# A state-space block on one core: B and C from one 128-row product, one of delta's casts moved to ScalarE

## Chip, cores and metric

One NeuronCore of one Trainium2 chip runs the whole program. The metric is device time in microseconds (us) of one execution.

## What is computed

Input x is 4 batches x 2048 tokens x 256 channels. Cut to what the change touches, with 512 inner channels and 64 states:

```python
xn    = layernorm(layernorm(x)) ; xi, z = split(xn @ W_in)
u     = silu(causal_conv4(xi) + conv_b)
x_dbl = u @ W_xproj                     # 16 + 64 + 64 columns
dt_r, B, C = x_dbl[:, :16], x_dbl[:, 16:80], x_dbl[:, 80:144]
delta = softplus(dt_r @ W_dt + b_dt)
h_t   = h_{t-1} * exp(delta_t * A) + (delta_t * u_t) B_t ;  y_t = h_t . C_t
out   = x + (y + u * D) * silu(z) @ W_out   # then a second residual block
```

## The kernel before

Four stages follow one another, each a block of five instruction streams that meet at its end: norm, **project** (the one that changes), scan, output. The scan reads from DRAM what the project stage stored.

The project stage (`project_stage`, from L343) walks over 16 tiles of 512 tokens (four per batch). `over_tiles` writes four tiles into a hardware loop over the first three batches and writes the last four out after it. All streams work on several tiles at once:

- **SyncE** issues every store. One `step` does `turn_stores` (the parts of delta*u, five stores of 1 MiB, L468; the parts of B, 0.5 MiB, L471; C, 0.25 MiB, L474), then `front_stores` (silu(z) and u, 1 MiB each), then `back_stores` (eight stores of 0.5 MiB of delta's three bf16 parts, L459), which waits for `d3_done` of the tile before. That is 11.75 MiB per tile.
- **TensorE**: per tile eight column blocks of `W_in` (`front`, L503) alternate with transposes of delta*u and B (`turn`, L537); then `back`: the 16 rows of dt_r (L510), four products with `W_dt` (L520), and two products of 128 rows (L510 again). The first of these has B twice, the second C twice, because `w_x` holds the columns of B and of C two times.
- **ScalarE** empties PSUM: `xi` (L576), turned parts (L624, L630), silu(z) (L579), u (L586), dt_r (L597), v (L601); then softplus's functions over 2048 columns: Abs (L604), Exp (L606), Ln (L608), the last two each behind a table load; last the copies `b_in` (L611) and `c_out` (L614).
- **VectorE**: `softplus` (L675 to L687), the convolution of the tile two ahead (`front`, L659 and L662), then `split`: x is cut into three bf16 parts, by cast, subtract, cast, subtract, for delta (into `dparts`) and then for delta*u (into `uparts`); then `split_b` the same for B. L675 is the first operation of a tile, and it waits for Exp of that tile (L606) and for `d3_done`.

Below, T*n* is the start of L675 of tile *n*, and T*n*+x a moment x us later.

Of the kernel before, what the change touches and what calls it, by code (L numbers as in the profile page):

```python
# [22 lines left out]
ALU = mybir.AluOpType  # L23
# [5 lines left out]
P = 128  # L29
# [7 lines left out]
TW = 512  # L37
# [305 lines left out]
def project_stage(nc, d, xnT):  # L343

    with ExitStack() as ctx:  # L345
# [6 lines left out]
        w_in = sb("p_w_in", [P, KD, 2 * DI])  # L352
        w_x = sb("p_w_x", [P, MI, RANK + 4 * NS])
        w_dt = sb("p_w_dt", [RANK, DI])
# [7 lines left out]
        dtr = sb("p_dtr", [RANK, TW])  # L362
        b_in = sb("p_b_in", [P, TW])
# [3 lines left out]
        c_out = sb("p_c_out", [P, TW])  # L367
        u_turn = sb("p_u_turn", [P, PARTS, SUB, DI])
# [42 lines left out]
        turns_stored = [sem(f"turns_stored{j}") for j in range(4)]  # L411
        n_weights = 10

# [19 lines left out]
        def _(sp):  # L433
            wx = d["W_xproj"].rearrange("(m p) n -> p m n", p=P)
            sp.dma_start(w_in[:, :, :], d["W_in"].rearrange("(k p) n -> p k n", p=P)).then_inc(weights, 16)
            sp.dma_start(w_x[:, :, 0:RANK], wx[:, :, 0:RANK]).then_inc(weights, 16)
            for r in range(4):
                at, frm = RANK + NS * r, RANK + NS * (r // 2)
                sp.dma_start(w_x[:, :, at:at + NS], wx[:, :, frm:frm + NS]).then_inc(weights, 16)
            sp.dma_start(w_dt[:, :], d["W_dt"]).then_inc(weights, 16)  # L440
# [50 lines left out]
            sp.wait_ge(dparts_stored, 16 * NCB * (NT + 1))  # L491
            sp.wait_ge(c_stored, 16 * (NT + 1))
            for j in range(4):
# [3 lines left out]
        def _(pe):  # L497
# [9 lines left out]
            def back(i, c, b):  # L507
                def rows(bank, lo, n):
                    for m in range(MI):
                        last = nc.tensor.matmul(bk_bank[0:n, bank, :], w_x[:, m, lo:lo + n], u[:, c % 2, m, :],  # L510
                                                start=(m == 0), stop=(m == MI - 1))
                    last.then_inc(back_ready, 1)

                pe.wait_ge(u_ready, i * 4 + 8)
                pe.wait_ge(back_read, i * 7 + 7)
                rows(2, 0, RANK)
                for m in range(MI):

                    pe.wait_ge(back_read, i * 7 + (8, 8, 9, 10)[m])
# [37 lines left out]
        def _(act):  # L557
            act.sem_inc(in_read, 2)
            act.sem_inc(back_read, 7)
            act.sem_inc(u_ready, 4)  # L560
# [8 lines left out]
            def front(i, m):  # L569
# [19 lines left out]
            def step(i, c, b, ahead1, ahead2):  # L589
# [4 lines left out]
                if ahead1:  # L594
                    middle(*ahead1)
                act.wait_ge(back_ready, i * 7 + 1)
                nc.scalar.activation(dtr[:, :], bk_bank[0:RANK, 2, :], ACT.Identity).then_inc(back_read, 1)  # L597
                act.wait_ge(delta_done, i + 1)
                for m in range(MI):
                    act.wait_ge(back_ready, i * 7 + 2 + m)  # L600
                    nc.scalar.activation(v[:, m, :], bk_bank[:, (3, 2)[m % 2], :], ACT.Identity,  # L601
                                         bias=b_dt[:, m:m + 1]).then_inc(back_read, 1)
                act.wait_ge(back_read, i * 7 + 12)
                nc.scalar.activation(ex[:, :, :], v[:, :, :], ACT.Abs).then_inc(abs_done, 1)  # L604
# [3 lines left out]
                nc.scalar.activation(lw[:, :, :], w1[:, :, :], ACT.Ln).then_inc(ln_done, 1)  # L608
                act.wait_ge(back_ready, i * 7 + 6)
                act.wait_ge(br_done, i + 1)  # L610
                nc.scalar.activation(b_in[:, :], bk_bank[:, 0, :], ACT.Identity).then_inc(back_read, 1)  # L611
                act.wait_ge(c_stored, i * 16 + 16)
                act.wait_ge(back_ready, i * 7 + 7)
                nc.scalar.activation(c_out[:, :], bk_bank[:, 1, :], ACT.Identity).then_inc(back_read, 1)  # L614

            def take_turn(i, g):
# [9 lines left out]
                else:  # L626
                    n, places = ((2, (0, 1, 2)), (1, (6, 7)))[g - 6]
                    for at in places:
                        src = turn_bank[:, g % 2, 0:n * SUB * P].rearrange("p (c s m) -> p s c m", s=SUB, m=P)
                        nc.scalar.activation(b_turn[:, :, at:at + 3 * n - 2:3, :], src[:, :, :, 0:NS],  # L630
                                             ACT.Identity).then_inc(turn_read, 1)

            for m in range(8):
                front(0, m)
            middle(0, 0, 0)
            over_tiles(act, step)
            for i in (NT, NT + 1):
                for g in range(8):
                    take_turn(i, g)

        @block.vector
        def _(dve):
            dve.sem_inc(delta_done, 1)
            nc.vector.memset(uparts[:, :, :, :], 0.0).then_inc(cleared, 1)
            nc.vector.memset(b_parts[:, :, :], 0.0).then_inc(cleared, 1)
            nc.vector.memset(dparts[:, :, :, :], 0.0).then_inc(cleared, 1)
            nc.vector.memset(c_out[:, :], 0.0).then_inc(cleared, 1)
            nc.vector.memset(xi[:, :, 0:TAPS - 1], 0.0).then_inc(xi_free, 1)
# [40 lines left out]
            def split(i):  # L689
                for src, rest, parts, free, first, whole, one, left, two, three, had in (  # L690
                        (lw, w1, dparts, (dparts_stored, i * (16 * NCB) + 16 * NCB), delta_done, i + 2, d1_done, dr_done,
                         d2_done, d3_done, 1),
                        (du, du, uparts, (turned, i * 8 + 16), du_done, i + 3, u1_done, ur_done, u2_done, u3_done, 2)):
                    dve.wait_ge(first, whole)
                    dve.wait_ge(*free)
                    nc.vector.tensor_copy(parts[:, 0], src[:, :, :]).then_inc(one, 1)
                    dve.wait_ge(one, i + 1)
                    nc.vector.tensor_tensor(rest[:, :, :], src[:, :, :], parts[:, 0], ALU.subtract).then_inc(left, 1)
                    dve.wait_ge(left, i + 1)
                    nc.vector.tensor_copy(parts[:, 1], rest[:, :, :]).then_inc(two, 1)  # L700
                    dve.wait_ge(two, i + 1)
                    nc.vector.tensor_tensor(parts[:, 2], rest[:, :, :], parts[:, 1], ALU.subtract).then_inc(three, 1)

            def split_b(i):
                dve.wait_ge(back_read, i * 7 + 13)
                dve.wait_ge(turned, i * 8 + 16)
                dve.wait_ge(b3_done, i + 2)
                nc.vector.tensor_copy(b_parts[:, 0], b_in[:, :]).then_inc(b1_done, 1)
                dve.wait_ge(b1_done, i + 1)
                nc.vector.tensor_tensor(b_rest[:, :], b_in[:, :], b_parts[:, 0], ALU.subtract).then_inc(br_done, 1)  # L710
                dve.wait_ge(br_done, i + 2)
                nc.vector.tensor_copy(b_parts[:, 1], b_rest[:, :]).then_inc(b2_done, 1)
                dve.wait_ge(b2_done, i + 1)
                nc.vector.tensor_tensor(b_parts[:, 2], b_rest[:, :], b_parts[:, 1], ALU.subtract).then_inc(b3_done, 1)

            def step(i, c, b, ahead1, ahead2):
# [4 lines left out]
                split(i)  # L721
                split_b(i)

            front(0, 0, 0)
# [739 lines left out]
```

## Time and profile before

| what | value |
|---|---|
| three runs, us | 5814.91, 5815.9, 5816.22 (median 5815.9) |
| profiled execution, us | 5813.2, of which the trace's span is 5811.4 |
| busy over the span | VectorE 95%, TensorE 90%, ScalarE 60%, GpSimd 39% |
| 50 to 850 us (holds the project stage) | VectorE 707 of 800 us, TensorE 675, ScalarE 563; DMA share 0.82 |
| 900 to 5400 us (inside the scan) | VectorE 4426 of 4500 us; DMA share 0.26 |

The DMA share is the mean busy share of the 16 DMA engines; where all work without a gap this profile shows 1.02 or 1.03. PEclk is the granted share of TensorE's 2.4 GHz. Rows of the order-of-time view read: start us, duration us, engine, line, operation, output and inputs, count, and in brackets the idle time before and what ended it.

### The profile page before, as it was taken

The page shows a single profiled execution, that of the slowest core. Times are in us where ns is not written, and L with a number is a line of the kernel's source. Part 1 is how long each engine was busy: PE and PEld are TensorE (multiplying, and loading weights), DVE is VectorE, ACT ScalarE, POOL GpSimd, SP SyncE. Part 2 cuts the span into 40 slices and gives each one's busy share as a digit, 9 for nine tenths or more (in the row PEclk, how much of TensorE's full clock was granted, in tenths as well). Part 3 has the DMA queues.
Part 4 walks back from the last instruction along what each step waited for, and adds up shares of the span by engine and source line. Part 5 has one row for each costly group of instructions (what it writes and reads, how often), then busy time and mean ns, then how long its engine had stood idle before and what let it go on. Part 6 is the DMA issues. An engine that isn't in the chain of part 4 may idle for free. (4 is left out here: it accounts for less than half of the span.)

```text
span 5811.4 us, 149606 instructions
## 1 busy us (share of the span) xinstructions
PE 5241.6 (90%) x38780; PEld 2478.7 (43%) x38780; DVE 5505.2 (95%) x3555; ACT 3494.6 (60%) x8238; POOL 2262.3 (39%) x6777
## 2 busy tenths in 40 slices
PE   5999779999999999999999999999999999997999
PEld 3344334444444444444444444444444444435666
DVE  5999989999999999999999999999999999995776
ACT  6777656666666666666666666666666666652333
POOL 2000034444444444444444444444444444440111
PEclk9999889999999999999999999999999999998999
DMA  7999942222222222222222222222222222224342
GB/s 245 332 321 337 344 111 53 54 54 55 54 52 53 54 54 54 54 52 53 54 54 55 54 52 53 54 55 54 54 52 54 53 55 54 54 44 147 115 141 73
DMA packets 1105518, 547.25 MB, mean 94 GB/s; under 512 B 753744, under 2 KB 1015056, under 8 KB 1105056
## 3 DMA queue, kind: packets, MB, share of 16 engines
q1 hardware_dynamic: 1093776, 533.89, 34.4%
q10 hardware_dynamic: 11664, 12.52, 0.6%
q8 instruction: 25, 0.41, 0.0%
q14 instruction: 53, 0.43, 0.0%
HBM read 296.83 MB, written 249.82 MB: 94 GB/s over the span
## 5 line engine op out<-in xcount | busy, mean ns | idle before, releaser
L997 DVE TENSOR_TENSOR_SCAN s_h<-s_decay,s_ubank 128x1024 f32<-128x1024 f32 x2048 | 4460.9, 2272 | 11.5 <-ACT s_ubank L962 11.2
L949 ACT ACTIVATE s_decay<-s_abank 128x512 f32<-128x512 f32 x4096 | 2210.4, 595 | 4.8 <-PE s_abank L887 1.4
L872 PE MATMUL s_ybank<-s_h,s_window 128*8 128x256 f32 x16416 | 1948.2, 602 | 1.9 <-DVE s_h L997 1.9
L913 PE MATMUL s_ubank<-s_x,s_w 128*128 128x256 bf16 x8192 | 1245.7, 275 | 375.5 <-DVE s_h L997 375.3
L1033 POOL TENSOR_TENSOR s_carry<-s_decay,s_h 128x64 f32<-128x64 f32 x2032 | 879.5, 433 | 1752.2 <-ACT s_decay L949 1576.4
L962 ACT ACTIVATE s_ubank<-s_seed 128x64 f32<-128x64 f32 x2048 | 478.3, 234 | 1703.2 <-PE s_ubank L913 1311.6
L887 PE MATMUL s_abank<-xnT,s_a 128*128 128x256 bf16 x8192 | 1254.9, 274 | 33.2 <-DMA s_w<-scratch_b_rows 30.1
L913 PEld LDWEIGHTS s_ubank<-s_x,s_w 128*128 128x128 bf16 x8192 | 675.7, 98 | 1197.7 <-DVE s_h L997 1096.5
L887 PEld LDWEIGHTS s_abank<-xnT,s_a 128*128 128x128 bf16 x8192 | 758.4, 98 | 195.8 <-ACT s_decay L949 35.7
L872 PEld LDWEIGHTS s_ybank<-s_h,s_window 128*8 128x8 f32 x16416 | 376.9, 97 | 839.6 <-issue 730.6
L1037 POOL TENSOR_TENSOR s_seed<-s_carry,s_first 128x64 f32<-128x64 f32 x2048 | 656.7, 321 | 164.3 <-ACT s_first L955 4.0
L1039 POOL TENSOR_TENSOR s_decay<-s_none 128x64 f32<-128x64 f32 x2048 | 617.3, 301 | 0.0
L503 PE MATMUL p_in<-xnT,p_w_in 128*128 (+1 forms) x512 | 252.4, 619 | 32.5 <-ACT p_xi L576 21.5
L1021 POOL TENSOR_TENSOR s_window<-s_c,s_none 64x32 f32<-64x32 f32 x512 | 129.9, 254 | 367.3 <-PE s_ybank L872 347.2
L1007 POOL MEMSET s_h<- 128x4096 f32 x1 | 3.5, 3511 | 663.6 <-POOLq L345 663.6
L1204 PE MATMUL o_gu<-o_xparts,o_wgu 128*128 128x512 bf16 x1152 | 257.8, 381 | 1.1 <-POOL o_xparts L1416 1.1
L897 PEld LDWEIGHTS s_firstbank<-s_x,s_w 128*128 128x128 bf16 x512 | 48.8, 95 | 444.0 <-issue 441.7
L1270 ACT ACTIVATE o_sg<-o_gu 128x512 f32<-128x512 f32 x96 | 57.4, 598 | 271.3 <-PE o_gu L1204 271.2
L510 PE MATMUL p_bk<-p_u,p_w_x 128*128 128x512 f32 (+1 forms) x384 | 203.4, 687 | 0.0
L955 ACT ACTIVATE s_first<-s_firstbank 128x256 f32<-128x256 f32 x512 | 203.3, 397 | 0.0
L939 ACT ACTIVATE s_y<-s_ybank 128x256 f32<-128x256 f32 x514 | 198.5, 386 | 6.8 <-PE s_ybank L872 6.8
L897 PE MATMUL s_firstbank<-s_x,s_w 128*128 128x512 bf16 x512 | 199.5, 390 | 2.0 <-DMA s_x<-scratch_u_rows 1.3
(135 smaller groups left out, 3098.2 us busy)
## 6 DMA issues: line engine op xcount, KB each, us to landing
s_x<-scratch_u_rows SPq DMA_DIRECT2D x4096, 32.0 KB
scratch_u_rows<-p_u_turn SPq DMA_DIRECT2D x90, 1024.0 KB, 6.6
scratch_delta_rows<-p_dparts SPq DMA_DIRECT2D x136, 512.0 KB, 6.2
xnT<-scratch_delta_rows SPq DMA_DIRECT2D x1024, 64.0 KB, 2.7
scratch_y<-s_y SPq DMA_DIRECT2D x1036, 16.0 KB
scratch_sz<-p_sz SPq DMA_DIRECT2D x16, 1024.0 KB, 6.2
scratch_u<-p_u SPq DMA_DIRECT2D x16, 1024.0 KB, 7.9
s_w<-scratch_b_rows SPq DMA_DIRECT2D x256, 64.0 KB, 2.4
```

Source lines behind the costliest of these rows:

```text
L503: last = nc.tensor.matmul(in_bank[:, m % 2, :], w_in[:, k, m * P:(m + 1) * P], xnT[:, k, bass.ds(i * TW, TW)], start=(k == 0), stop=(k == ...
L872: last = nc.tensor.matmul(y_bank[32 * ct:32 * ct + WIN, 1 - x, :], window[:, of, (at + t) * WIN:(at + t + 1) * WIN], H[:, 1 - x, :, t], st ...
L887: last = nc.tensor.matmul(a_bank[:, b, jj], a_w[:, half, j, :], x1[:, g, :, half, j, s * T:(s + 1) * T], start=True, stop=True)
L897: nc.tensor.matmul(first_bank[:, :, :], w2[:, g, 4 * s + 2 * x, :], x2[:, s, 0, 2 * x], start=True, stop=True).then_inc(first_ready, 1)
L913: last = nc.tensor.matmul(dst.rearrange("p q (a t) -> p a q t", t=2), w2[:, g, 4 * s + 2 * x + e, :], x2[:, s, :, 2 * x + e, q:q + 32, :], ...
L949: nc.scalar.activation(dst.rearrange("p x q t -> p q x t"), a_bank[:, b].rearrange("p j r (x t) -> p (j r) x t", x=2), ACT.Exp).then_inc(e ...
L962: nc.scalar.activation(u_bank[:, k % 2, :, 0], seed[:, k % CPS, :], ACT.Identity).then_inc(seeded, 1)
L997: nc.vector.tensor_tensor_scan(H[:, x, PT * p:PT * p + PT, :].rearrange("p q t -> p (q t)"), decay[:, x * (1 + c % 2), p].rearrange("p q t ...
L1033: nc.gpsimd.tensor_tensor(carry[:, k % CPS, :], decays, before, ALU.mult).then_inc(carried, 1)
L1037: nc.gpsimd.tensor_tensor(seed[:, k % CPS, :], carry[:, k % CPS, :], first[:, x, PT * p:PT * p + PT], ALU.add).then_inc(carried, 1)
L1039: nc.gpsimd.tensor_tensor(decays, none[:, :], none[:, :], ALU.mult).then_inc(carried, 1)
L1204: last = nc.tensor.matmul(gu[:, m % 2, r, :], wgu[:, r, kk, m * P:(m + 1) * P], xparts[:, part, kk, :], start=(n == 0), stop=(n == 3 * KD ...
```

## The change

`w_x` holds B and C once, so one product of 128 rows gives B in rows 0 to 63 and C in rows 64 to 127. One copy (`bc_in`) takes the place of `b_in` and `c_out`. C goes to DRAM twice from the upper 64 rows, 0.125 MiB each. The cast into `dparts[:, 1]` is done on ScalarE after the copies of v (`second_delta`), and the subtraction that reads it is the last operation of VectorE's tile (`split_last`). SyncE's `back_stores` waits for both. The weights come by 6 transfers in place of 10.

```diff
         w_x = sb("p_w_x", [P, MI, RANK + 2 * NS])
...
-            sp.dma_start(w_x[:, :, 0:RANK], wx[:, :, 0:RANK]).then_inc(weights, 16)
-            for r in range(4):
-                at, frm = RANK + NS * r, RANK + NS * (r // 2)
-                sp.dma_start(w_x[:, :, at:at + NS], wx[:, :, frm:frm + NS]).then_inc(weights, 16)
+            sp.dma_start(w_x[:, :, :], wx[:, :, :]).then_inc(weights, 16)
...
             def back_stores(i, c, b):
+                sp.wait_ge(d2_done, i + 1)
                 sp.wait_ge(d3_done, i + 1)
...
-                    sp.dma_start(d["C"][:, rows], c_out[:, :]).then_inc(c_stored, 16)
+                    for h in range(2):
+                        sp.dma_start(d["C"][h * NS:h * NS + NS, rows], bc_in[NS:P, :]).then_inc(c_stored, 16)
...
                 rows(0, RANK, 2 * NS)
-                rows(1, RANK + 2 * NS, 2 * NS)
...
+            def second_delta(i):
+                act.wait_ge(dr_done, i + 1)
+                nc.scalar.activation(dparts[:, 1], w1[:, :, :], ACT.Identity).then_inc(d2_done, 1)
...
+                second_delta(i)
+                act.wait_ge(back_read, i * 6 + 11)
                 nc.scalar.activation(ex[:, :, :], v[:, :, :], ACT.Abs).then_inc(abs_done, 1)
...
-                nc.scalar.activation(b_in[:, :], bk_bank[:, 0, :], ACT.Identity).then_inc(back_read, 1)
-                act.wait_ge(c_stored, i * 16 + 16)
-                act.wait_ge(back_ready, i * 7 + 7)
-                nc.scalar.activation(c_out[:, :], bk_bank[:, 1, :], ACT.Identity).then_inc(back_read, 1)
+                act.wait_ge(c_stored, i * 32 + 32)
+                nc.scalar.activation(bc_in[:, :], bk_bank[:, 0, :], ACT.Identity).then_inc(back_read, 1)
...
+            act.wait_ge(cleared, 4)
...
             for i in (NT, NT + 1):
                 for g in range(8):
                     take_turn(i, g)
+                if i == NT:
+                    second_delta(NT)
...
+            nc.vector.memset(w1[:, :, :], 0.0).then_inc(dr_done, 1)
...
+            def split_last(i):
+                dve.wait_ge(d2_done, i + 2)
+                nc.vector.tensor_tensor(dparts[:, 2], w1[:, :, :], dparts[:, 1], ALU.subtract).then_inc(d3_done, 1)
...
                 split(i)
                 split_b(i)
+                split_last(i)
```

**VectorE, the end of a tile**, before (L696 to L702 are the splits of delta and delta*u, L708 to L714 B's, L675 the next tile):

```order
L696 CAST p_dparts<-p_lw 128x2048
L698 TENSOR_TENSOR p_w<-p_lw,p_dparts 128x2048
L700 CAST p_dparts<-p_w 128x2048
L702 TENSOR_TENSOR p_dparts<-p_w,p_dparts 128x2048
L695 ISA
L696 CAST p_uparts<-p_du 128x2048
```

and the same engine and place with the change, where lines have moved (L723 is `split_last`, L679 the next tile's first operation):

```order
L696 CAST p_dparts<-p_lw 128x2048
L698 TENSOR_TENSOR p_w<-p_lw,p_dparts 128x2048
L700 ISA
L701 CAST p_uparts<-p_du 128x2048
L703 TENSOR_TENSOR p_du<-p_du,p_uparts 128x2048
L705 CAST p_uparts<-p_du 128x2048
L707 TENSOR_TENSOR p_uparts<-p_du,p_uparts 128x2048
L710 ISA
L713 CAST p_b_parts<-p_bc_in 128x512
L715 TENSOR_TENSOR p_b_rest<-p_bc_in,p_b_parts 128x512
L717 CAST p_b_parts<-p_b_rest 128x512
L719 TENSOR_TENSOR p_b_parts<-p_b_rest,p_b_parts 128x512
L723 TENSOR_TENSOR p_dparts<-p_w,p_dparts 128x2048
L679 TENSOR_SCALAR p_w<-p_ex 128x2048
```

One cast has gone, and the operation that completes `dparts` stands behind the other splits.

**ScalarE, from the last copy of v to the next tile**, with the change:

```order
L602 ACTIVATE p_v<-p_bk,p_b_dt 128x512
L580 ACTIVATE p_dparts<-p_w 128x2048
L605 REGISTER_ALU
L606 ACTIVATE p_ex<-p_v 128x2048
L608 ACT_TABLE_LOAD
L608 ACTIVATE p_ex<-p_ex 128x2048
L610 ACT_TABLE_LOAD
L610 ACTIVATE p_lw<-p_w 128x2048
L611 REGISTER_ALU
L614 ACTIVATE p_bc_in<-p_bk 128x512
```

The cast (L580) stands ahead of Abs and Exp; one copy follows Ln where there were two.

## Rows read from the trace of the kernel before

**Rows 1.** Order of time, VectorE, tile 2 and the start of tile 3

```profile
218.15 1.22 DVE L675 TENSOR_SCALAR p_w<-p_ex 128x2048 f32<-128x2048 f32 x1
...
238.43 1.23 DVE L696 CAST p_dparts<-p_lw 128x2048 bf16<-128x2048 f32 x1
...
242.02 1.23 DVE L700 CAST p_dparts<-p_w 128x2048 bf16<-128x2048 f32 x1
243.28 2.29 DVE L702 TENSOR_TENSOR p_dparts<-p_w,p_dparts 128x2048 bf16<-128x2048 f32 x1
...
254.79 1.22 DVE L675 TENSOR_SCALAR p_w<-p_ex 128x2048 f32<-128x2048 f32 x1
```

**Rows 2.** Order of time, SyncE (SPq: its queue), two groups of store issues

```profile
209.10 10.01 SPq L459 DMA_DIRECT2D scratch_delta_rows<-p_dparts  x8
...
675.32 5.33 SPq L468 DMA_DIRECT2D scratch_u_rows<-p_u_turn  x5
```

**Rows 3.** Busy time by stretch: length; PE, PEld, DVE, ACT, POOL busy; PEclk; DMA share; GB/s

```profile
226.20:260.00 33.80, 30.66 (x110) 12.86 (x109) 33.29 (x34) 24.40 (x31) 0.00 (x0) 0.95 1.02 363
...
675.00:748.00 73.00, 31.60 (x189) 17.45 (x188) 60.89 (x33) 34.50 (x44) 0.00 (x0) 0.71 1.02 357
748.00:750.00 2.00, 0.00 (x0) 0.00 (x0) 0.24 (x1) 0.00 (x0) 0.41 (x1) 0.50 0.24 79
```

**Rows 4.** Order of time, ScalarE, over the same tile as Rows 1

```profile
221.70 0.59 ACT L614 ACTIVATE p_c_out<-p_bk 128x512 f32<-128x512 f32 x1
222.18 0.60 ACT L576 ACTIVATE p_xi<-p_in 128x512 f32<-128x512 f32 x1
...
244.26 0.69 ACT L601 ACTIVATE p_v<-p_bk,p_b_dt 128x512 f32<-128x512 f32 x1 [0.17 <-PE p_bk L520]
...
248.21 1.91 ACT L606 ACTIVATE p_ex<-p_ex 128x2048 f32<-128x2048 f32 x1
```

**Rows 5.** Order of time, TensorE, the same tile

```profile
222.83 1.98 PE L503 MATMUL p_in<-xnT,p_w_in 128*128 x4 [1.51 <-ACT p_xi L576]
...
244.16 8.83 PE L510 MATMUL p_bk<-p_u,p_w_x 128*128 128x512 f32 x16
```

**Rows 6.** Order of time, a tile with less room: Exp, and VectorE's next tile

```profile
328.60 1.91 ACT L606 ACTIVATE p_ex<-p_ex 128x2048 f32<-128x2048 f32 x1
...
333.54 1.22 DVE L675 TENSOR_SCALAR p_w<-p_ex 128x2048 f32<-128x2048 f32 x1
```

**Rows 7.** Order of time, the two tiles that hold the loop's jump back

```profile
265.05 3.78 PE L503 MATMUL p_in<-xnT,p_w_in 128*128 x4 [7.09 <-ACT p_xi L576]
...
294.17 1.91 ACT L606 ACTIVATE p_ex<-p_ex 128x2048 f32<-128x2048 f32 x1
...
296.91 1.23 DVE L675 TENSOR_SCALAR p_w<-p_ex 128x2048 f32<-128x2048 f32 x1
...
446.43 1.91 ACT L606 ACTIVATE p_ex<-p_ex 128x2048 f32<-128x2048 f32 x1
...
449.62 1.22 DVE L675 TENSOR_SCALAR p_w<-p_ex 128x2048 f32<-128x2048 f32 x1
```

**Rows 8.** Order of time, the start of the stage: SyncE and TensorE

```profile
85.86 4.06 SPq L439 DMA_DIRECT2D p_w_x<-in_W_xproj  x4
...
93.81 12.79 PE L503 MATMUL p_in<-xnT,p_w_in 128*128 128x512 f32 x24 [10.65 <-DMA p_b_dt<-in_b_dt]
```

**Rows 9.** Order of time, VectorE, the first operation of tiles 0, 14 and 15

```profile
144.02 1.23 DVE L675 TENSOR_SCALAR p_w<-p_ex 128x2048 f32<-128x2048 f32 x1 [14.85 <-ACT p_ex L606]
...
669.33 1.22 DVE L675 TENSOR_SCALAR p_w<-p_ex 128x2048 f32<-128x2048 f32 x1
...
696.19 1.22 DVE L675 TENSOR_SCALAR p_w<-p_ex 128x2048 f32<-128x2048 f32 x1
```

**Rows 10.** TensorE near the end: an idle time, and a stretch behind it

```profile
674.44 0.62 PE L537 MATMUL p_turn<-p_ident,p_uparts 128*128 128x128 bf16 x8 [3.87 <-ACT p_u_turn L624]
...
676.00:678.00 2.00, 1.80 (x17) 1.39 (x16) 1.90 (x2) 1.79 (x3) 0.00 (x0) 0.50 0.89 330
```

More of the change, by code:

```diff
@@ L352, in project_stage @@
         w_in = sb("p_w_in", [P, KD, 2 * DI])
-        w_x = sb("p_w_x", [P, MI, RANK + 4 * NS])
+        w_x = sb("p_w_x", [P, MI, RANK + 2 * NS])
         w_dt = sb("p_w_dt", [RANK, DI])
@@ L362, in project_stage @@
         dtr = sb("p_dtr", [RANK, TW])
-        b_in = sb("p_b_in", [P, TW])
+        bc_in = sb("p_bc_in", [P, TW])
         b_rest = sb("p_b_rest", [P, TW])
@@ L366, in project_stage @@
         b_turn = sb("p_b_turn", [P, SUB, NCB, NS], BF16)
-        c_out = sb("p_c_out", [P, TW])
         u_turn = sb("p_u_turn", [P, PARTS, SUB, DI])
@@ L411, in project_stage @@
         turns_stored = [sem(f"turns_stored{j}") for j in range(4)]
-        n_weights = 10
+        n_weights = 6
         block = ctx.enter_context(nc.Block())
@@ L491, in _ @@
             sp.wait_ge(dparts_stored, 16 * NCB * (NT + 1))
-            sp.wait_ge(c_stored, 16 * (NT + 1))
+            sp.wait_ge(c_stored, 32 * (NT + 1))
             for j in range(4):
@@ L514, in back @@
                 pe.wait_ge(u_ready, i * 4 + 8)
-                pe.wait_ge(back_read, i * 7 + 7)
+                pe.wait_ge(back_read, i * 6 + 6)
                 rows(2, 0, RANK)
                 for m in range(MI):
-                    pe.wait_ge(back_read, i * 7 + (8, 8, 9, 10)[m])
+                    pe.wait_ge(back_read, i * 6 + (7, 7, 8, 9)[m])
                     nc.tensor.matmul(bk_bank[:, (3, 2)[m % 2], :], w_dt[:, m * P:(m + 1) * P], dtr[:, :],
@@ L558, in _ @@
             act.sem_inc(in_read, 2)
-            act.sem_inc(back_read, 7)
+            act.sem_inc(back_read, 6)
             act.sem_inc(u_ready, 4)
@@ L595, in step @@
                     middle(*ahead1)
-                act.wait_ge(back_ready, i * 7 + 1)
+                act.wait_ge(back_ready, i * 6 + 1)
                 nc.scalar.activation(dtr[:, :], bk_bank[0:RANK, 2, :], ACT.Identity).then_inc(back_read, 1)
@@ L599, in step @@
                 for m in range(MI):
-                    act.wait_ge(back_ready, i * 7 + 2 + m)
+                    act.wait_ge(back_ready, i * 6 + 2 + m)
                     nc.scalar.activation(v[:, m, :], bk_bank[:, (3, 2)[m % 2], :], ACT.Identity,
                                          bias=b_dt[:, m:m + 1]).then_inc(back_read, 1)
-                act.wait_ge(back_read, i * 7 + 12)
+                second_delta(i)
+                act.wait_ge(back_read, i * 6 + 11)
                 nc.scalar.activation(ex[:, :, :], v[:, :, :], ACT.Abs).then_inc(abs_done, 1)
@@ L608, in step @@
                 nc.scalar.activation(lw[:, :, :], w1[:, :, :], ACT.Ln).then_inc(ln_done, 1)
-                act.wait_ge(back_ready, i * 7 + 6)
+                act.wait_ge(back_ready, i * 6 + 6)
                 act.wait_ge(br_done, i + 1)
-                nc.scalar.activation(b_in[:, :], bk_bank[:, 0, :], ACT.Identity).then_inc(back_read, 1)
-                act.wait_ge(c_stored, i * 16 + 16)
-                act.wait_ge(back_ready, i * 7 + 7)
-                nc.scalar.activation(c_out[:, :], bk_bank[:, 1, :], ACT.Identity).then_inc(back_read, 1)
+                act.wait_ge(c_stored, i * 32 + 32)
+                nc.scalar.activation(bc_in[:, :], bk_bank[:, 0, :], ACT.Identity).then_inc(back_read, 1)
             def take_turn(i, g):
@@ L646, in _ @@
             nc.vector.memset(dparts[:, :, :, :], 0.0).then_inc(cleared, 1)
-            nc.vector.memset(c_out[:, :], 0.0).then_inc(cleared, 1)
+            nc.vector.memset(bc_in[:, :], 0.0).then_inc(cleared, 1)
             nc.vector.memset(xi[:, :, 0:TAPS - 1], 0.0).then_inc(xi_free, 1)
@@ L689, in split @@
             def split(i):
[L690 to L702, printed above, removed]
+                dve.wait_ge(delta_done, i + 2)
@@ new lines, in split @@
+                dve.wait_ge(dparts_stored, i * (16 * NCB) + 16 * NCB)
+                nc.vector.tensor_copy(dparts[:, 0], lw[:, :, :]).then_inc(d1_done, 1)
+                dve.wait_ge(d1_done, i + 1)
+                nc.vector.tensor_tensor(w1[:, :, :], lw[:, :, :], dparts[:, 0], ALU.subtract).then_inc(dr_done, 1)
+                dve.wait_ge(du_done, i + 3)
+                dve.wait_ge(turned, i * 8 + 16)
+                nc.vector.tensor_copy(uparts[:, 0], du[:, :, :]).then_inc(u1_done, 1)
@@ L704, in split_b @@
+                dve.wait_ge(u1_done, i + 1)
+                nc.vector.tensor_tensor(du[:, :, :], du[:, :, :], uparts[:, 0], ALU.subtract).then_inc(ur_done, 1)
+                dve.wait_ge(ur_done, i + 1)
+                nc.vector.tensor_copy(uparts[:, 1], du[:, :, :]).then_inc(u2_done, 1)
+                dve.wait_ge(u2_done, i + 1)
+                nc.vector.tensor_tensor(uparts[:, 2], du[:, :, :], uparts[:, 1], ALU.subtract).then_inc(u3_done, 1)
             def split_b(i):
-                dve.wait_ge(back_read, i * 7 + 13)
+                dve.wait_ge(back_read, i * 6 + 12)
@@ L706, in split_b @@
                 dve.wait_ge(turned, i * 8 + 16)
                 dve.wait_ge(b3_done, i + 2)
-                nc.vector.tensor_copy(b_parts[:, 0], b_in[:, :]).then_inc(b1_done, 1)
+                nc.vector.tensor_copy(b_parts[:, 0], bc_in[:, :]).then_inc(b1_done, 1)
                 dve.wait_ge(b1_done, i + 1)
-                nc.vector.tensor_tensor(b_rest[:, :], b_in[:, :], b_parts[:, 0], ALU.subtract).then_inc(br_done, 1)
+                nc.vector.tensor_tensor(b_rest[:, :], bc_in[:, :], b_parts[:, 0], ALU.subtract).then_inc(br_done, 1)
```

## Prediction

> **What bounds the kernel now.** I read the busy shares first: VectorE leads in the stretch that holds the project stage. Whether it is the bound tile by tile shows in its order of time. Tile 2 runs from 218.15 to 254.79, 36.6 us, with no bracket (no idle time) in it [rows 1]. ScalarE's Exp, which the next L675 needs, ends at 250.12, so VectorE was 4.67 us from having to wait [rows 4, 1]. Other tiles have less: in the one that ends at 333.54 Exp ends at 330.51, a room of 3.03 us [rows 6]. Of the twelve tiles before tile 14 without a jump of the loop, the rest lie between these two or near them. The two with the jump have 0.83 and 1.28 us [rows 7].
>
> The DMA engines are the second resource to read, and the page's average hides them. From 226.2 to 260.0 they worked without a gap: 33.8 us at 363 GB/s, which is one tile's 11.75 MiB [rows 3]. So a tile has 36.6 us of VectorE and 33.8 us of DMA work; the DMA engines rest 2.8 us. This changes at the end. Tiles 14 and 15 have no convolution ahead of them and take VectorE 26.9 us [rows 9], less than the DMA work. From 675.0 the DMA engines never rest until about 748.5 [rows 3], 25 MiB (three times the 5 MiB of delta\*u and 0.5 of B, twice C and delta's 4). **The stage therefore ends when its last store has landed, not when VectorE is done.** In VectorE's time that is T14+79.2.
>
> **The change, part by part.**
>
> *VectorE's tile.* The cast goes: from its start to the next operation 1.26 us [rows 1]. The subtraction is moved, not shortened. New tile: 35.4 us. Twelve tiles without a jump between T0 and T14: 12 x 1.26 = 15.1 us.
>
> *Is Exp still in time?* ScalarE gets a 2048-column Identity. The trace has none; the nearest row is Exp over the same elements, 1.91 us, and I take it (bounds: VectorE's cast of the same data, 1.23; a fourfold 0.69 of the v copy, 2.8) [rows 1, 4]. It needs no table of its own, since Identity already runs beside Silu and Ln here. It waits for the first subtraction of delta, which ends at T+23.9, while the v copies end at T+26.8, so the wait is covered. One copy at the end goes: from L614 to L576 0.48 us [rows 4]. From ScalarE's first xi copy to the last v the pace is TensorE's, which the dropped product (behind the v products in order) does not touch. So Exp ends 1.91 - 0.48 = 1.43 us later against T, and VectorE wants it 1.26 sooner: the room shrinks by 2.7 us, from 4.7 and 3.0 to 2.0 and 0.3. It stays positive, barely. I allow 0.18 us of waiting per tile: 2.2 us given back.
>
> *The two tiles with the jump* have no room to lose. There Exp sets the pace: 1.43 - 0.83 = +0.6 us and 1.43 - 1.28 = +0.1 us [rows 7]. Nothing gained, 0.7 lost.
>
> *TensorE.* Half of the sixteen records of 8.83 us go, 4.4 us per tile [rows 5]. It lies in no chain: TensorE already waited 1.51 us for ScalarE's first copy [rows 5], and this wait grows to some 3.5 us. I price it at nothing. What covers it is VectorE's tile; the second rival says what it can cost.
>
> *Queues behind the new waits.* `split_last` waits for ScalarE's cast (done by about T+28.3) at T+33.1: no wait. `bc_in` takes over the wait for C's store, which stood one copy later; at the rate of [rows 3] that store's turn comes after 4 MiB of delta, 5 of delta\*u and 0.5 of B, so it has landed by about T+30, and `bc_in` runs at about T+38.5. SyncE issues one store more per tile. Behind its new wait on `d2_done` stand only delta's stores, and `d3_done` is later anyhow.
>
> *Delta's stores move.* Before, `dparts` was complete at 245.5, T+27.4, and SyncE issued eight stores over 10 us (the group of the tile before begins at 209.10, the moment it could) [rows 1, 2]. Now it is complete at the tile's end, so these 4 MiB start at the next T. In the steady stretch this costs nothing: the DMA work of 33.8 us still fits in 35.4, its rest shrinks to 1.6 us, and the stores have landed at about T+13.5 when `dparts` is wanted again at T+20.3 [rows 1]. **In the tail it costs in full.** Before, tile 13's delta had gone out when the unbroken stretch began, with the first delta\*u store at 675.32 [rows 2], T14+6. Now the stretch begins under 1 us after T14, but with 4 MiB more in it. At the same 26.2 MB in 73.5 us these take 11.7 us. End: T14 + 0.8 + 11.7 + 73.5 = T14+86.0, against T14+79.2: 6.8 us lost. VectorE waits about 2 us for `dparts` in tiles 14 and 15 (wanted at T+10.5 where no convolution is done, free at T+12.5), which is hidden: delta of tile 14 is complete at T14+27.6 and its turn on the DMA engines comes at T14+29.5.
>
> *Start.* Four transfers of `W_xproj` took 4.06 us to issue [rows 8] and one remains; TensorE's first product waited for the weights. Gain 0 to 4 us; I take 2.5, since the large `W_in` still has to land and the longer clearing of `w1` holds ScalarE near that. The first `second_delta` adds 1.9 to the chain before T0. Net 0.6 gained.
>
> **Sum.** 15.1 - 2.2 - 0.7 + 0.6 = 12.8 us earlier at T14; minus 6.8 in the tail: 6.0 us. The scan and output stages are unchanged and shift. The sum is made against the profiled execution (5813.2 us); the median of the runs shown is 5815.9, 2.7 above it. Against the median: 5809.9, said as **5810 us**. A measurement of this kernel tells about 0.2% (11.6 us) from no change, so this is a gain too small to be told.
>
> **Rivals.**
>
> *The tail does not charge for delta's stores*, because the DMA engines have room there or because stores of delta run faster than the average. Against it: 73 us with a share of 1.02 [rows 3]. Then 12.8 us, or up to 17 with no waits at Exp and a full gain at the start: 5799 to 5803.
>
> *The softplus chain becomes the bound.* TensorE's wait before the third column block grows to 3.5 us. After an idle time of 7.09 us the four records behind it took 3.78 us in place of 1.98 [rows 7, 5], and after one of 3.87 us the granted clock was 0.50, the 1.2 GHz level, about 2 us later [rows 10]. A fall in each tile puts 1.8 us into the chain from xi to v: Exp would end at T+35.2 in the tile with most room and T+36.8 in that with least. With tiles of 36.0 the stage gives and takes the same; with all at 36.8 the twelve tiles lose 2, and with the jumps, start and tail the kernel is 9 us slower. The point from which it decides is a tile of 36.0 us. I put its time at 5820. The Trainium skill says the same in "TensorE: Matmul & The Clock Gate", section "Why this matters for your kernels": gaps between bursts of matmuls send the array back to half clock. By that rule this change, which takes work from TensorE alone, makes the remaining work slower. For it speaks the row after 3.87 us; against it, that TensorE is busy for most of the rest of a tile and has waited 1.5 us in each tile without such a loss [rows 5].
>
> *The DMA engines become the bound in the steady stretch.* Work of 33.8 us leaves 1.6; two stores of C from 64 partitions, or a late delta, could take that. A tile of 36 us gives about no change, 5816.
>
> **Chances.** Forecast 0.55; tail free 0.18; softplus chain 0.20; DMA bound 0.07. The range reaches from 5801 (most of the second case) to 5821 (the third in its middle). Faster by over 0.2% (below 5804.3) is most of the tail-free case: 0.17. Slower by over 0.2% (above 5827.5) needs every tile over 37 us or some loss in the scan that I don't see: 0.05. Within 0.2%: 0.78.
>
> **What would show it.** Right: VectorE's T to T is 35.4 us with no or short idle time before its first operation; Exp ends 0 to 2 us before it; the Identity cast takes 1.9 us; TensorE has one product of 128 rows less; SyncE issues delta's stores at T; the last unbroken DMA stretch is some 85 us in place of 73; T14 is 12 to 13 us earlier and the stage's end only 6. Wrong: idle time at the first operation released by Exp in most tiles; a DMA share under 1 in the tail; or the scan stage of another length than before.

## The result, and the profile after

| | before | with the change |
|---|---|---|
| median of 5 runs, us | 5815.9 (5814.15 to 5816.22) | 5989.3 (5984.83 to 5993.16) |
| ratio | | 1.030, 95% interval 1.029 to 1.031 |
| span of the profiled execution, us | 5811.4 | 5988.0 |

The kernel is 3% slower; 5810 had been predicted, and 5821 was the top of the range. The first question is in which stage the time lies. The rows are the start of the scan stage (L983 before, L993 after), the first and last scans, and one of the first operations of the output stage. VectorE before, in order of time:

```profile
749.76 0.48 DVE L983 MEMSET s_window<- 128x512 f32 x1 [9.55 <-PEq L345]
771.52 4.46 DVE L997 TENSOR_TENSOR_SCAN s_h<-s_decay,s_ubank 128x1024 f32<-128x1024 f32 x2 [9.95 <-ACT s_ubank L962]
...
5229.48 4.44 DVE L997 TENSOR_TENSOR_SCAN s_h<-s_decay,s_ubank 128x1024 f32<-128x1024 f32 x2
5260.30 1.41 DVE L1314 SCALAR_TENSOR_TENSOR o_yg<-o_u,o_dskip,o_tr 128x512 f32<-128x512 f32 x2 [26.38 <-DMA o_sz<-scratch_sz]
```

and with the change:

```profile
735.95 0.48 DVE L993 MEMSET s_window<- 128x512 f32 x1 [12.86 <-PEq L345]
757.63 4.46 DVE L1007 TENSOR_TENSOR_SCAN s_h<-s_decay,s_ubank 128x1024 f32<-128x1024 f32 x2 [9.87 <-ACT s_ubank L972]
...
5404.01 4.44 DVE L1007 TENSOR_TENSOR_SCAN s_h<-s_decay,s_ubank 128x1024 f32<-128x1024 f32 x2
...
5435.40 1.40 DVE L1324 SCALAR_TENSOR_TENSOR o_yg<-o_u,o_dskip,o_tr 128x512 f32<-128x512 f32 x2 [26.95 <-DMA o_sz<-scratch_sz]
```

The project stage ends 13.8 us earlier, and the first scan starts 13.9 us earlier. From the first scan to the end of the last it was 4462.4 us and is 4650.8: **188.4 us more in a stage of which no line was edited**. The way from there to the end of the program grew by 2.1 us. -13.9 + 188.4 + 2.1 = 176.6 us, the difference between the spans.

**Inside the scan.** The page's row of the scan, before and then after:

```profile
L997 DVE TENSOR_TENSOR_SCAN s_h<-s_decay,s_ubank 128x1024 f32<-128x1024 f32 x2048 | 4460.9, 2272 | 11.5 <-ACT s_ubank L962 11.2
```

```profile
L1007 DVE TENSOR_TENSOR_SCAN s_h<-s_decay,s_ubank 128x1024 f32<-128x1024 f32 x2048 | 4473.2, 2262 | 187.4 <-ACT s_ubank L972 186.9
```

One scan is no longer than it was (2262 ns, before 2272); VectorE waits 187.4 us ahead of them in place of 11.5. That is 175.9 of the 188.4 us; the other 12.3 stand in the busy time, and why is not shown. VectorE's order of time shows the rhythm:

```profile
2059.37 69.80 DVE L1007 TENSOR_TENSOR_SCAN s_h<-s_decay,s_ubank 128x1024 f32<-128x1024 f32 x32 [2.51 <-ACT s_ubank L972]
2131.51 69.80 DVE L1007 TENSOR_TENSOR_SCAN s_h<-s_decay,s_ubank 128x1024 f32<-128x1024 f32 x32 [2.34 <-ACT s_ubank L972]
```

One wait of some 2.5 us in every 32 scans here, and over the stage 188.4 / 64 = 2.9 us in each 32. That is one turn of a hardware loop: each engine's scan loop takes four chunks of 8 scans a turn (`over_chunks`, 64 turns). The releaser ScalarE is not the cause; the waits between 1000 and 4000 us, longest totals (line waited for: us, times, longest), lead further back:

```profile
PE s_ubank L923 <- DMA s_x<-scratch_u_rows: 120.9, 41, 3.3
DVE s_h L1007 <- ACT s_ubank L972: 116.5, 59, 3.3
```

Neither row is among the longest waits of the kernel before. TensorE waits 41 times in some 41 turns for a load, and SyncE issues the loads. SyncE's order of time over the same turn:

```profile
2027.26 7.67 SPq L854 DMA_DIRECT2D s_x<-scratch_u_rows  x16
2035.23 1.69 SPq L833 DMA_DIRECT2D scratch_y<-s_y  x4
2040.09 5.95 SPq L842 DMA_DIRECT2D xnT<-scratch_delta_rows  x8
...
2072.27 1.70 SPq L833 DMA_DIRECT2D scratch_y<-s_y  x4
2074.35 6.37 SPq L842 DMA_DIRECT2D xnT<-scratch_delta_rows  x8
```

and in the kernel before:

```profile
2031.83 1.70 SPq L823 DMA_DIRECT2D scratch_y<-s_y  x4
2033.91 5.91 SPq L832 DMA_DIRECT2D xnT<-scratch_delta_rows  x8
...
2066.67 1.73 SPq L823 DMA_DIRECT2D scratch_y<-s_y  x4
2069.14 5.99 SPq L832 DMA_DIRECT2D xnT<-scratch_delta_rows  x8
```

Stores of y are followed by loads of delta twice a turn, once inside the loop's body and once across its jump. Before, the two gaps are 0.4 and 0.7 us. After, one is 0.4 and the other, across the jump, 3.2 us. Over the 41 turns from 1000 to 4000 us the gap has a mean of 3.1 us. In the turn shown, three groups of issues are 0.4 to 0.5 us longer than before as well (`xnT` at 2074.35: 6.37 us, before 5.91), so the gap is most of the 2.9 us and not all. What goes on in it is in the DMA queues' rows for 1000 to 4000 us (packets, MB, share), before and then after:

```profile
q14 instruction: 10, 0.08, 0.0%
```

```profile
q14 instruction: 216, 1.77, 0.2%
```

The queue that brings instructions moved 10 packets in 3000 us, and now 216, about 5 in each turn, of 8.2 KB each. So code is loaded again at each turn. Two of the packets lie in the gap itself, from 2036.9 to 2040.1 us:

```profile
q14 instruction: 2, 0.02, 1.6%
```

**The project stage** did better than predicted. VectorE's first operation (L679) of tiles 2, 3, 4, 14 and 15 with the change, and the operation ahead of tile 2's:

```profile
212.68 2.28 DVE L723 TENSOR_TENSOR p_dparts<-p_w,p_dparts 128x2048 bf16<-128x2048 f32 x1
215.07 1.23 DVE L679 TENSOR_SCALAR p_w<-p_ex 128x2048 f32<-128x2048 f32 x1
...
250.51 1.23 DVE L679 TENSOR_SCALAR p_w<-p_ex 128x2048 f32<-128x2048 f32 x1
...
289.17 1.23 DVE L679 TENSOR_SCALAR p_w<-p_ex 128x2048 f32<-128x2048 f32 x1 [1.68 <-ACT p_ex L608]
...
647.45 1.23 DVE L679 TENSOR_SCALAR p_w<-p_ex 128x2048 f32<-128x2048 f32 x1 [0.87 <-ACT p_ex L608]
...
677.06 1.23 DVE L679 TENSOR_SCALAR p_w<-p_ex 128x2048 f32<-128x2048 f32 x1
```

Tile 2 is 35.44 us (36.64 in [rows 1]), and T14 is 647.45 where it was 669.33 [rows 9]. The tail is longer: from T14 to the scan stage's first operation 88.5 us, before 80.4. Its stretches (columns as in [rows 3]) are full to the end:

```profile
648.00:734.00 86.00, 32.72 (x188) 18.98 (x188) 63.59 (x33) 42.33 (x49) 0.00 (x0) 0.62 1.00 349
734.00:736.00 2.00, 0.00 (x0) 0.00 (x0) 0.05 (x1) 0.00 (x0) 0.22 (x1) 0.50 0.37 125
```

### The profile page after: what moved, and what is told of

The parts are those of the page before. It is cut to its first block and busy times, and to the rows that moved or that the text cites. A ratio compares the mean times of both kernels' runs of the same rounds, so it can differ in the third digit from the quotient of the medians.

```text
span 5988.0 us, 148894 instructions
## 1 busy us (share of the span) xinstructions
PE 5188.4 (87%) x38171; PEld 2476.3 (41%) x38652; DVE 5499.0 (92%) x3540; ACT 3510.9 (59%) x8239; POOL 2261.9 (38%) x6777
## 5 line engine op out<-in xcount | busy, mean ns | idle before, releaser
L1007 DVE TENSOR_TENSOR_SCAN s_h<-s_decay,s_ubank 128x1024 f32<-128x1024 f32 x2048 | 4473.2, 2262 | 187.4 <-ACT s_ubank L972 186.9
L923 PE MATMUL s_ubank<-s_x,s_w 128*128 128x256 bf16 x8192 | 1270.5, 279 | 569.6 <-DVE s_h L1007 318.5
L897 PE MATMUL s_abank<-xnT,s_a 128*128 128x256 bf16 x8192 | 1300.1, 278 | 49.3 <-DMA s_w<-scratch_b_rows 34.9
L923 PEld LDWEIGHTS s_ubank<-s_x,s_w 128*128 128x128 bf16 x8192 | 692.3, 99 | 1135.8 <-DVE s_h L1007 951.2
L1214 PEld LDWEIGHTS o_gu<-o_xparts,o_wgu 128*128 128x128 bf16 x1152 | 113.2, 98 | 130.7 <-issue 4.3
L1423 POOL TENSOR_TENSOR o_rstd<-o_veps,o_half 128x4 f32<-128x4 f32 x16 | 16.1, 1008 | 355.0 <-DVE o_veps L1345 355.0
```

Of the source, the lines that this page charges most:

```text
L897: last = nc.tensor.matmul(a_bank[:, b, jj], a_w[:, half, j, :], x1[:, g, :, half, j, s * T:(s + 1) * T], start=True, stop=True)
L923: last = nc.tensor.matmul(dst.rearrange("p q (a t) -> p a q t", t=2), w2[:, g, 4 * s + 2 * x + e, :], x2[:, s, :, 2 * x + e, q:q + 32, :], ...
L1007: nc.vector.tensor_tensor_scan(H[:, x, PT * p:PT * p + PT, :].rearrange("p q t -> p (q t)"), decay[:, x * (1 + c % 2), p].rearrange("p q t ...
L1214: last = nc.tensor.matmul(gu[:, m % 2, r, :], wgu[:, r, kk, m * P:(m + 1) * P], xparts[:, part, kk, :], start=(n == 0), stop=(n == 3 * KD ...
```

## The experiments

Two theories on the 3%. **Place:** the edit changed how many instructions stand ahead of the scan loops, and on one engine the loop now lies where its jump back needs code to be fetched anew. Counted in the built programs (what the kernel's code is turned into, one list of instructions for each engine), SyncE's scan loop is 220 instructions long and starts 334 instructions into its program before, 352 with the change. **Work:** something the edit does (the doubled stores of C, the data's layout, an engine's late finish) slows the loads of the scan. To move a loop without doing any work I put waits that have long been met in front of it; two of them make one instruction. In SyncE's program they stand behind the last stores of the project stage:

```diff
             turn_stores(NT + 1, True)
+            for _ in range(184):        # a_sp92: 92 instructions; the number varies
+                sp.wait_ge(cleared, 4)
```

**First TensorE**, whose program lost products and weight loads: 64 small products, with their loads 128 instructions, are added behind its project work, on the changed kernel and on the one before.

```diff
+            for n in range(64):
+                nc.tensor.matmul(bk_bank[:, 1, 0:32], ident[:, :], ident[:, 0:32], start=True, stop=True)
```

> The change, with 64 small bf16 products (128 TensorE instructions: a weight load and a matmul each) into the unused bank 1 at the end of TensorE's project stream, so that the scan loop stands where it stood before. Theory 'place of the code': about 5802 us (5816 less the 13.9 us that the project stage ends earlier), VectorE's idle time before the scan operation about 12 us as before in place of 187, and the instruction queue q14 back from 358 packets to some 50. Rival 'data' (the scan's loads or buffers are slower because the project stage stores or allocates otherwise): still about 5989 us, 187 us idle.

> The kernel before, computing just as before, with the same 64 products at the end of TensorE's project stream: the scan loop moves by 128 instructions, by as much as in the change but the other way. Theory 'place of the code', if what matters repeats every 256 instructions: about 6000 us (5816 + 187), q14 some 350 packets. Rival 'data': 5816 us, at most 5 us more. If the theory holds but the places do not repeat so: between, or 5816.

Measured: 5983.2, ratio 1.029 (1.028 to 1.031), with 181.7 us of idle time at the scan, and 5815.7, ratio 1.000 (0.999 to 1.001). TensorE's place is not it: neither putting its loop back nor moving it in the kernel before changes the scan.

**Half the change each.** `bc_only` is the kernel before with the one product, `bc_in` and the two stores of C; VectorE keeps its cast. `cast_only` is the kernel before with the cast on ScalarE, `split_last` and the later stores.

> The kernel before with one product, one copy and two stores of C alone; delta's cast stays on VectorE. Theory 'place of the code': TensorE's stream is as short as in the change, so the scan waits 187 us in all: 5995 to 6003 us. Rival 'the cast on ScalarE did it': about 5816 us. In the project stage VectorE's tile stays 36.6 us.

> The kernel before with the cast on ScalarE, split_last and the later stores of delta alone; two products and two copies stay. Theory 'place of the code': TensorE's stream is that of before, the scan as before; the project stage: VectorE's tile 35.4 to 36 us, tail 7 us longer in VectorE's time, so 5800 to 5812 us. Rival 'the cast did it': 5980 us or more.

Measured: 5977.4, 1.028 (1.026 to 1.030), and 5983.3, 1.029 (1.028 to 1.031). Each half, with no edited operation in common, does all the damage (177.5 and 171.0 us of idle time at the scan), so the work of neither is likely to be the cause. `cast_only` also has TensorE's program as it was before, which rules its place out once more. What the halves share is a start of SyncE's scan loop at 343.

**Nine instructions on SyncE**, in the kernel before, as 18 waits; the loop moves from 334 to 343 and nothing else changes.

> The kernel before, computing the same, with 18 more waits on SyncE that are long met (9 instructions, two waits in one) at the end of its project stream, behind the last stores. SyncE's scan loop of 220 instructions then stands at instruction 343 of the built program, as in the two halves of the change, in place of 334. Theory 'place of SyncE's loop': some 5975 to 6000 us, a gap of 3 to 4 us on SyncE between the last store of y and the first load of delta once per turn of the loop (0.4 before), and 350 or more packets on q14. Rival 'the project stage's data or stores': 5815 us.

Measured: **5996.1, ratio 1.031 (1.030 to 1.033)**. The page's rows of the queue and of the scan:

```profile
q14 instruction: 368, 3.01, 0.2%
...
L999 DVE TENSOR_TENSOR_SCAN s_h<-s_decay,s_ubank 128x1024 f32<-128x1024 f32 x2048 | 4473.1, 2263 | 178.8 <-ACT s_ubank L964 178.1
```

Nine instructions that do nothing, executed once, cost 182 us. This is the loss of the change in a kernel without the change; no theory of work is left.

**And 92 to undo it**, in the changed kernel; then 220.

> The change with 92 more such instructions at that place: the loop starts at 444. Theory 'place of SyncE's loop', if places repeat every 128 instructions: as good as before, 5802 us and q14 near 50 packets. If they repeat every 256 only: still some 5985 us. Rival 'data': 5989 us.

> The change with 220 more: the loop starts at 572, which is 18 less than 334 + 256. Theory 'place of SyncE's loop': 5802 us whether places repeat every 128 or every 256 instructions (up to 8 us more if the waits themselves are not covered by the last stores). Rival 'data', or a longer stream being the worse: 5989 us or more.

Measured: 5802.6, ratio 0.998 (0.997 to 0.999), and 5806.5, 0.9985 (0.9975 to 0.9994). With 92:

```profile
q14 instruction: 44, 0.36, 0.0%
...
L1009 DVE TENSOR_TENSOR_SCAN s_h<-s_decay,s_ubank 128x1024 f32<-128x1024 f32 x2048 | 4460.7, 2260 | 11.5 <-ACT s_ubank L974 11.4
```

The 188 us are gone with 92 instructions more. With 220 the kernel is 4 us slower than with 92: VectorE waits 18.0 us for the scan stage to begin in place of 13.3, so that many waits are no longer free. The gap across SyncE's jump is back to that of before:

```profile
2049.82 1.70 SPq L835 DMA_DIRECT2D scratch_y<-s_y  x4
2052.26 5.93 SPq L844 DMA_DIRECT2D xnT<-scratch_delta_rows  x8
```

**What each half is worth in a good place**: 101 instructions on SyncE put both loops at 444, where the 92 put the changed kernel's.

> One product, one copy and two stores of C alone, with 101 instructions of met waits on SyncE so that its scan loop starts at instruction 444, the good place of a_sp92. Theory 'each half by itself is harmless, the place of SyncE's loop is all': VectorE's tile stays 36.6 us, the wait at the project loop's jump on ScalarE is absent (as in bc_only), the weights land 1 to 2 us sooner: 5804 to 5810 us. Rival 'one product costs in the scan by itself': 5977 us as in bc_only.

> The cast on ScalarE alone, SyncE's loop at 444 as well. Theory 'place': VectorE's tile 35.4 to 36.5 us (two copies stay, so Exp has 0.5 us less room than in the change), ScalarE's wait at the project loop's jump 2.5 us each in place of 4.1, delta's stores late in the tail: 5806 to 5812 us. Rival: 5983 us as in cast_only.

Measured: 5803.4, 0.998 (0.997 to 0.999), and 5806.7, 0.9985 (0.998 to 0.999). With `bc_sp101` VectorE's regular tiles are 36.63 us as before, and its gain is in the two tiles with the jump, 37.22 and 37.20 us where they had been 42.12 and 42.81. With `cast_sp101` the regular tiles are 35.44 and those with the jump 40.66 and 40.70. Together (`a_sp92`) the halves give 11 us, hardly more than either alone: their gains in the tiles reach T14 (25.8 us earlier than before), and the tail takes more of it back: 9.1 us, where it takes 1.3 in `bc_sp101` and 8.4 in `cast_sp101`. What `bc_sp101` gains is a matter of place as well, as the next runs show: ScalarE has a pause at the jump before, and none in that run.

**ScalarE's jump.** Why did the tiles with the jump become shorter? ScalarE's order of time at the jump of its project loop, before:

```profile
258.34 0.59 ACT L614 ACTIVATE p_c_out<-p_bk 128x512 f32<-128x512 f32 x1
263.10 1.28 ACT L576 ACT_TABLE_LOAD   x1 [4.17 <-issue]
```

and with the change:

```profile
253.59 0.58 ACT L614 ACTIVATE p_bc_in<-p_bk 128x512 f32<-128x512 f32 x1
254.19 1.28 ACT L573 ACT_TABLE_LOAD   x1
```

A pause of 4.17 us, for nothing the profile shows, is gone. If that too is a matter of place, instructions on ScalarE bring it back: `a_act6` is `a_sp92` with six more ahead of ScalarE's project loop.

> a_sp92 with 6 more instructions of met waits on ScalarE ahead of its project loop (the loop at 190 to 454 of the built program in place of 184 to 448; before 183 to 451). Theory 'ScalarE's wait of 4.1 us at the loop's jump is also a matter of place, and the change lost it by chance': the wait is back at both jumps, tiles 3 and 7 are 3 to 5 us longer each, 5809 to 5812 us. Rival 'the wait went for another reason, such as the removed copy': no wait, 5802.6 us.

Measured: 5809.5, 0.999 (0.998 to 1.000), 7 us slower than `a_sp92`. The pause is back at 3.10 us, with a second one of 3.07 us behind it, and the tiles with the jump are 40.04 and 42.31 us:

```profile
256.95 1.28 ACT L575 ACT_TABLE_LOAD   x1 [3.10 <-issue]
...
261.91 1.02 ACT L626 ACTIVATE p_u_turn<-p_turn 128x1024 f32<-128x1024 bf16 x1 [3.07 <-issue]
```

The start alone does not decide it. ScalarE's project loop runs from instruction 183 to 451 of its built program before, from 184 to 448 in the changed kernel, from 190 to 454 in `a_act6` and from 184 to 456 in `cast_sp101`. The second has no pause at its jumps and the others have one, although the second and the last start at the same instruction. The instruction queue says the same: a kernel with this pause has about 10 packets more than the like kernel without it (53 to 55 against 44 and 45, and 368 against 358 to 361), for two jumps. That is some 5 packets a jump, as at SyncE's.

**A better version.** The tail takes back part of what the tiles gain, because delta's stores start only when `split_last` has run. It can run ahead of B's splits; SyncE's 92 instructions stay.

```diff
                 split(i)
-                split_b(i)
                 split_last(i)
+                split_b(i)
```

> a_sp92 with split_last ahead of split_b, so that delta's third part is complete 2.2 us sooner in each tile. If the project stage's end is set by the DMA engines, which start the last unbroken stretch with delta's stores of tile 13: that stretch starts and ends about 2.2 us sooner, 5800.4 us against 5802.6, the tile's length unchanged. If the tail is set by something else: 5802.6 us.

Measured: **5793.0 us, ratio 0.996 (0.995 to 0.998)**, the fastest of all and 22 us under the kernel before on the same chip (5814.8). The regular tiles are 35.24 us, with no wait at Exp in any of them, and SyncE issues delta's stores ahead of the next tile's first operation:

```profile
209.87 2.28 DVE L725 TENSOR_TENSOR p_dparts<-p_w,p_dparts 128x2048 bf16<-128x2048 f32 x1
...
214.32 1.22 DVE L681 TENSOR_SCALAR p_w<-p_ex 128x2048 f32<-128x2048 f32 x1
```

```profile
212.37 9.14 SPq L456 DMA_DIRECT2D scratch_delta_rows<-p_dparts  x8
```

The project stage ends 4.6 us earlier than in `a_sp92`, where 2.2 had been expected, and the medians are 9.6 us apart. Why it gains more than its 2.2 us, and why no tile waits for Exp any more, is not shown.

**Which places are bad?** Only SyncE's number varies from here. My first rule was that the body must lie within two pieces of 128 instructions; it calls for a slow 412.

> The change with 60 more instructions of met waits on SyncE: its scan loop starts at 412, between the bad 352 and the good 444. The starts tried give, by their remainder to 128: good 78 (334) and 60 (444, 572), bad 87 (343) and 96 (352). A loop of 220 instructions lies within two pieces of 128 for 36 to 37 starts in 128, so the good remainders are a band of that width whose upper end is 78 to 86: it begins at 42 to 50. 412 has the remainder 28. Theory 'it must lie within two pieces of 128': bad, some 5985 us. Rival 'some more distance is always good' : 5802 us.

Measured: 5801.3, 0.998 (0.997 to 0.999), with 44 packets. The rule fell. The rest are one execution each, enough for a step of 180 us.

> The changed kernel with 16 met waits' instructions on SyncE behind the project loop's last stores: its scan loop starts 368 instructions into SyncE's program (slow so far at 343 and 352, fast at 334, 412, 444 and 572). Bad band wider than this: about 5985 us, some 358 packets on the instruction queue, a pause of about 3 us at each turn of SyncE's scan loop. Band ended before 368: about 5800 us, some 45 packets.

> The same with 32 instructions, the scan loop at 384. Bad band wider than this: about 5985 us and some 358 packets. Band ended before 384: about 5800 us and some 45 packets. Together with the loop at 368 this gives the upper edge of the band between 352 and 412.

> The same with 128 instructions, the scan loop at 480 (352 + 128). If the bad places repeat every 128 instructions: about 5985 us and some 358 packets. If they repeat at a longer distance or not at all: about 5800 us and some 45 packets.

> The same with 256 instructions, the scan loop at 608 (352 + 256). If the bad places repeat every 256 instructions: about 5985 us and some 358 packets. If it is not the place modulo 256 (352 is a single edge of the program, or the distance is longer): about 5800 us and some 45 packets.

> The changed kernel with 160 instructions on SyncE behind the project loop's last stores: scan loop at 512. Slow so far at 343, 352, 368, 384, 480 and 608, fast at 334, 412, 444 and 572. If the place counts modulo 128 (slow from 87 through 0, fast from 28 to 78): 512 is 0, slow, about 5985 us and some 358 packets. If it counts modulo 256 (slow 87 to 128 and 224, fast 60 to 78 and 156 to 188), 512 is 0, between a slow and a fast place, and says where the edge lies.

> The same with 188 instructions: scan loop at 540, which is 28 modulo 128, as the fast 412 is: about 5800 us and some 45 packets. Modulo 256 it is 28, where nothing was tried: if it is slow, the distance is not 128.

All starts tried, with the remainder of the start by 128:

| start | remainder | time, us | packets of q14 |
|---|---|---|---|
| 412 (a_sp60) | 28 | 5801.3 | 44 |
| 540 (a_sp188) | 28 | 5800.2 | 45 |
| 444 (a_sp92) | 60 | 5802.6 | 44 |
| 572 (a_sp220) | 60 | 5806.5 | 45 |
| 334 (before) | 78 | 5815.9 | 53 |
| 343 (b_sp9) | 87 | 5996.1 | 368 |
| 352 (the change) | 96 | 5989.3 | 358 |
| 480 (a_sp128) | 96 | 5994.1 | 359 |
| 608 (a_sp256) | 96 | 5994.4 | 361 |
| 368 (a_sp16) | 112 | 5971.1 | 358 |
| 384 (a_sp32) | 0 | 5979.1 | 358 |
| 512 (a_sp160) | 0 | 5981.5 | 359 |

Remainders of 28 to 78 are good and 87 through 0 are bad, without an exception, and the last two runs (`a_sp160`, `a_sp188`) came out as this rule had said ahead. The loop has the same length in all of them, so its start and its end are not told apart here.

A packet is 8.2 KB. By the figures of the Trainium skill ("Runtime: NRT & Kernel Launch", section "Instruction fetch mechanics": blocks of 16 KiB hold 256 instructions) that is an estimated 128 instructions, which agrees with the repeat. The same section says that a taken branch whose target is outside the two blocks held forces a fetch before execution can go on. The pauses agree with that: 3.2 us with two packets in them. But by its figures a body of 220 instructions lies within the 512 that are held wherever it starts, if the chip's program is as long as the built one, so no place should have cost anything; here the measurement decides. Where the edges are between 78 and 87 and between 0 and 28, and why a body of this length needs some five packets a turn at a bad place, stays open.

## Why the prediction was wrong

**The step that failed** is one sentence of the sum: "The scan and output stages are unchanged and shift." Their lines are unchanged, but SyncE's scan loop was moved from 334 to 352 in its program, over an edge, and its jump back now pauses about 3 us in each of 64 turns: 188 us. The loss was in no term of the sum, and no rival had it; it stood only in the chance of 0.05, as "some loss in the scan that I don't see". The kernel before showed both sides: SyncE's jump without a pause, and ScalarE's with one of 4.17 us that the trace puts down to "issue". I had read the 7.09 us of the tile with the jump [rows 7] as a TensorE matter and did not ask what ScalarE did in it.

The rest, point by point:

- **VectorE's tile, right.** 35.4 us predicted and 35.44 measured wherever no wait stands ahead.
- **Waits at Exp, right in kind, too small.** The twelve regular tiles average 35.74 us: 0.3 us of waiting a tile, not 0.18. ScalarE's cast takes 1.90 us (1.91 said), and Exp of tile 2 ends 2.3 us before it is wanted (2.0 said). The excess goes with TensorE's clock, the mechanism of the rival in which the softplus chain becomes the bound. A tile without a wait, then the one before a wait of 1.40:

```profile
215.07:250.51 35.44, 31.36 (x119) 13.46 (x118) 34.85 (x33) 29.87 (x37) 0.00 (x0) 0.95 0.99 347
...
574.58:611.28 36.70, 32.45 (x115) 14.07 (x114) 34.82 (x33) 28.33 (x36) 0.00 (x0) 0.86 0.98 341
```

```profile
219.27 1.99 PE L501 MATMUL p_in<-xnT,p_w_in 128*128 x4 [2.66 <-ACT p_xi L573]
...
236.78 3.88 PE L518 MATMUL p_bk<-p_dtr,p_w_dt 16*128 16x512 f32 x8 [0.68 <-ACT p_dtr L598]
```

```profile
578.78 3.38 PE L501 MATMUL p_in<-xnT,p_w_in 128*128 128x512 f32 x4 [3.58 <-ACT p_xi L573]
...
597.98 5.73 PE L518 MATMUL p_bk<-p_dtr,p_w_dt 16*128 16x512 f32 x8 [0.68 <-ACT p_dtr L598]
```

  The clock's mean is 0.95 and 0.86. Behind the wait for ScalarE's first copy the four records take 1.99 us and 3.38, the products with `W_dt` 3.88 us and 5.73, and Exp ends 3.5 us later in its tile. It happens in some tiles, not in all, so that their mean of 35.74 us stays under the 36.0 from which it was to decide. `cast_sp101` keeps the second product: its twelve regular tiles have a clock of 0.90 or 0.95 and no wait at Exp, which speaks for a link from the dropped product to the waits. But `cast_only`, with the same project stage, has waits of 0.80 and 2.22 us in its last two regular tiles, and `a_early`, without the product, has tiles at 0.85 and no wait. So the link is likely, not shown. The section of the Trainium skill that the prediction names ("TensorE: Matmul & The Clock Gate", "Why this matters for your kernels") has gaps between bursts of matmuls as the cause of a lower clock; the two rows agree with it, and other tiles of the same kernel do not fall.
- **The two tiles with the jump, wrong by 10.7 us in the kernel's favour.** Predicted 0.7 us longer in sum; they are 38.66 and 36.28 us, 10.0 shorter. The step that failed here is "There Exp sets the pace: 1.43 - 0.83 = +0.6 us": it takes the rest of the tile as it was, and the pause of ScalarE at its jump, which had held Exp back, went. `a_act6` shows that this is a matter of place.
- **Start, right:** T0 is 0.4 us earlier (0.6 said).
- **T14**: 12.8 us earlier predicted, 21.9 measured. That is 11.5 from the regular tiles (12.9 said), 10.0 from the two with the jump, 0.4 from the start.
- **The tail, right:** 8.1 us lost against 6.8. The unbroken stretch is 86 us at 349 GB/s, as long as said; tile 14 took 29.6 us, not 27.6.
- **The stage's end**: 13.8 us earlier, 6 said. With SyncE's loop in a good place (`a_sp92`) the kernel takes 5802.6 us, which is inside the predicted range: the place of one loop is all that put the result outside it. The run nearest to what was priced is `a_act6`, in which ScalarE pauses at its jumps again: T14 is 13.4 us earlier (12.8 said), the stage's end 5.4 (6.0 said), and the kernel takes 5809.5 us (5810 said). So close a figure is partly luck: its two tiles with the jump are 2.6 us shorter in sum than before, not 0.7 longer, its regular tiles wait 0.4 us each, not 0.18, and its tail loses 8.1 us, not 6.8.

## What to carry to other kernels

Every instruction that an edit adds or takes, on any engine and in any earlier stage, moves the hardware loops behind it in that engine's program, and a loop's jump back can cost nothing or 3 to 4 us by where the loop lies. So in the profile of the kernel before, look at each engine's gap across each jump and at the packets of the instruction queue, and multiply a possible pause by the turns. When a stage slows whose code was not touched, compare these two first; met waits ahead of the loop move it, and while the places of the loops differ, the times of two kernels do not compare their work alone.

## What was not expected of the hardware

- Nine instructions executed once cost 182 us of 5814, through a loop of 64 turns behind them (5996.1 against 5814.2 on the same chip).
- SyncE does no arithmetic, and a pause of 3 us in each turn of 72 us, on an engine that only issues loads and stores, is seen in full on VectorE. From 1000 to 4000 us SyncE still waits 514 us for TensorE to free the buffers of `s_x` (521 before), so this idle time did not take up the pause.
- The bad places repeat after 128 instructions, and the good remainders that were tried span 50 of the 128.
- The clock of TensorE fell in some tiles of equal work and not in others (0.86 and 0.95).
